# One perceiver layer on one core: denominators of the self attention as a seventeenth value column, normalised on the way out of PSUM, and all engines' steps in a new order

## The reference

```python
q, k = rms_norm(q), rms_norm(k)                       # then rotary, then q * q_gain
scores = einsum('bqhgd,bkhd->bhgqk', qg, k) * scale   # 32 x 32 for a head and sequence
scores = where(causal, scores, -inf)
attn = softmax(scores, axis=-1)
y = einsum('bhgqk,bkhd->bqhgd', attn, v)              # 256 values of a position
return ternary_linear(rms_norm(y), w_proj)
```

## Time and profile before

| what | value |
|---|---|
| three runs, median (lowest, highest) | 593.45 us (590.78, 594.42) |
| the profiled execution, its own time | 593.49 us |
| its span, first to last instruction | 591.3 us |
| TensorE busy | 525.6 us, 89% |
| VectorE, ScalarE, GpSimd busy | 448.9, 424.2, 323.9 us |
| mean granted TensorE clock | 0.958 of 2.4 GHz |

### The profile page before, as it was taken

One profiled execution on the slowest core, in us unless ns is written; L12 is line 12 of the kernel. 1 busy time (PEld: TensorE's weight loads), 2 busy tenths in 40 slices (PEclk: granted clock), 3 DMA queues, 4 the chain that ended last, 5 costly groups with the idle time before them and its releaser, 6 DMA issues. The chain is left out here.

```text
span 591.3 us, 22164 instructions
## 1 busy us (share of the span) xinstructions
PE 525.6 (89%) x6950; PEld 437.1 (74%) x6950; DVE 448.9 (76%) x1389; ACT 424.2 (72%) x1208; POOL 323.9 (55%) x489
## 2 busy tenths in 40 slices
PE   5898989999999999999999999999999999975633
PEld 4686878787887878887887878887877878853422
...
PEclk9999999999999999999999999999999999996565
...
GB/s 249 172 111 76 157 2 112 75 34 97 43 99 54 77 74 63 84 31 115 27 90 54 84 69 70 75 36 118 25 85 53 101 16 99 20 25 7 21 9 9
DMA packets 42748, 41.60 MB, mean 70 GB/s; under 512 B 16080, under 2 KB 33488, under 8 KB 42704
## 3 DMA queue, kind: packets, MB, share of 16 engines
...
...
## 5 line engine op out<-in xcount | busy, mean ns | idle before, releaser
L883 ACT ACTIVATE pr<-sm,nb 128x257 f32<-128x257 f32 x256 | 129.0, 508 | 8.4 <-DVE nb L1122 7.5
L667 POOL TENSOR_TENSOR cTl<-cx,cTh 128x516 fp32r<-128x516 f32 x64 | 85.9, 1342 | 75.9 <-ACT cTh L779 75.9
L1122 DVE CUSTOM_DVE_ANT_0 sm<-x_ps,mbias 128x257 f32<-128x257 f32 x256 | 99.9, 421 | 27.4 <-PE x_ps L1423 24.0
L1433 PE MATMUL x_ps<-tab,pr 128*128 128x128 f32 x512 | 71.6, 274 | 0.7 <-DVE o L1153 0.4
L779 ACT ACTIVATE pt<-x_ps 128x512 f32<-128x512 f32 x112 | 64.9, 594 | 10.2 <-PE x_ps L1433 6.9
L779 ACT ACTIVATE kk<-x_ps 128x257 f32<-128x257 f32 x128 | 49.2, 387 | 29.5 <-PE x_ps L1320 29.5
L1320 PE MATMUL x_ps<-cTh,wkTh 128*128 128x258 f32 x256 | 60.2, 317 | 0.4 <-ACT pt L779 0.3
L1433 PEld LDWEIGHTS x_ps<-tab,pr 128*128 128x128 f32 x512 | 57.2, 141 | 4.4 <-issue 2.0
L676 POOL TENSOR_TENSOR sr<-sv,halfneg 128x20 f32<-128x20 f32 x16 | 56.7, 3543 | 1.3
L1320 PE MATMUL x_ps<-wvTh,cTh 128*128 128x256 f32 x256 | 56.8, 303 | 0.2
L1423 PE MATMUL x_ps<-kk,qbd 32*64 32x257 f32 x1024 | 44.3, 400 | 10.6 <-POOL qbd L688 5.8
...
## 6 DMA issues: line engine op xcount, KB each, us to landing
...
```

Of the source, the lines that this page charges most:

```text
L667: g.tensor_tensor(cxbuf(cT[1], b)[:, :, :], cx[:, b % BT, :, :], cxbuf(cT[0], b)[:, :, :].bitcast(F32), ALU.subtract).then_inc(A_ctl, 1)
L883: sc.activation(pr[:, b % 2, gr, :], sm[:, b % 2, gr, :], ACT.Exp, bias=nb[:, n:n + 1], scale=-1.0, accum_out=st[:, 0, b, gr:gr + 1]).then ...
L1122: v.tensor_tensor_reduce(out=sm[:, b % 2, gr, :], in0=xb(f"S{b}", gr)[:, 0:LK], in1=mbias[:, b, :], scale=1.0, scalar=0.1 * NEG, op0=ALU.a ...
L1433: last = tr(xb(f"PT{b}{c}")[:, gr * P:(gr + 1) * P], pr[:, b % 2, gr, c * P:(c + 1) * P], ident)
```

## The change

The values' block form vbd gets a seventeenth column in each group, which GpSimd fills once, before the passes, with the ones and zeros of the block pattern. The product D_PV is then 68 columns wide in place of 64, and each seventeenth holds the sum of the exponentials. D_dn and D_p3 are gone, with the buffers p3 and dn2; D_p4 transposes p2 itself. A new VectorE step D_ys takes the reciprocals of the 16 sums out of PSUM (strided) and multiplies the 256 values by them from PSUM into ys. ScalarE no longer copies ys; it squares and sums ys from SBUF. The bank of D_PV is free after B_ys in place of B_yss. ScalarE's exponential waits for the transpose (B_p4) of the tile before in place of the product p3. In the files line numbers differ by up to two.

All orders of `SCHEDULE` and the banks of `BANK` are new. Of the tables, the row of GpSimd for one pass, and TensorE's first row:

```diff
@@ SCHEDULE["pool"]["each"] @@
-            ("PX", 0), ("CL", 2), ("CL", 3), ("D_vbd",), ("Q_root",), ("B_root",), ("PX", 1), ("CL", 4),
+            ("CL", 2), ("CL", 3), ("B_root",), ("PX", 0), ("D_vbd",), ("PX", 1), ("CL", 4), ("Q_root",),
...
@@ SCHEDULE["pe"]["each"] @@
-            ("S", 0), ("K", 1, 0), ("K", 1, 1), ("C_xT",), ("B_st",), ("D_kT",), ("V", 1), ("B_O",), ("D_QT",),
+            ("B_st",), ("S", 0), ("K", 1, 0), ("K", 1, 1), ("V", 1), ("C_xT",), ("D_kT",), ("D_QT",), ("PT", 0, 0),
...
@@ perceiver: buffers, release @@
-        vbd = sb("vbd", [P, BT * KV, 4, HD])
-        soft = sb("soft", [P, 5, BT * KV * S])
-        s2, s3, p2, p3, p4 = (soft[:, n, :].rearrange("p (j k) -> p j k", k=S) for n in range(5))
+        vbd = sb("vbd", [P, BT * KV, 4, HD + 1])
+        soft = sb("soft", [P, 4, BT * KV * S])
+        s2, s3, p2, p4 = (soft[:, n, :].rearrange("p (j k) -> p j k", k=S) for n in range(4))
...
-            "D_S": (B_s2, 1, -2, 1), "D_PV": (B_yss, 1, -2, 1), "D_yT": (B_yTl, 1, -2, 1), "D_pj": (B_x2, 1, -2, 1),
+            "D_S": (B_s2, 1, -2, 1), "D_PV": (B_ys, 1, -2, 1), "D_yT": (B_yTl, 1, -2, 1), "D_pj": (B_x2, 1, -2, 1),
@@ GpSimd @@
+            g.tensor_copy(vbd[:, :, :, HD], m4.unsqueeze(1).to_broadcast([P, BT * KV, 4])).then_inc(W_set, 1)
...
                         g.tensor_tensor(
-                            vbd[:, :, :, :],
+                            vbd[:, :, :, 0:HD],
@@ ScalarE @@
                     elif k == "D_S":
                         act.wait_ge(B_s3, i1)
                         if due(i1 - 1):
-                            act.wait_ge(B_p3, i1 - 1)
+                            act.wait_ge(B_p4, i1 - 1)
                         sc.activation(p2[:, :, :], s3[:, :, :], ACT.Exp).then_inc(B_p2, 1)
                     elif k == "D_PV":
-                        act.wait_ge(B_pv, i1)
-                        if due(i1 - 1):
-                            act.wait_ge(B_yTp, i1 - 1)
-                        copy(ys[:, :], xb("D_PV")[:, 0:D]).then_inc(B_ys, 1)
+                        act.wait_ge(B_ys, i1)
                         if due(i1 - 1):
                             act.wait_ge(B_yv, i1 - 1)
-                        sc.activation(ysq[:, :], xb("D_PV")[:, 0:D], ACT.Square, accum_out=yss[:, :]).then_inc(B_yss, 1)
+                        sc.activation(ysq[:, :], ys[:, :], ACT.Square, accum_out=yss[:, :]).then_inc(B_yss, 1)
@@ VectorE @@
-                    elif k == "D_dn":
+                    elif k == "D_p4":
                         dve.wait_ge(B_p2, i1)
-                        v.tensor_reduce(dn2[:, :], p2[:, :, :], AX.X, ALU.add).then_inc(B_dn, 1)
-                        dve.wait_ge(B_dn, i1)
-                        v.reciprocal(rd2[:, :], dn2[:, :]).then_inc(B_rc2, 1)
-                    elif k == "D_p3":
-                        dve.wait_ge(B_rc2, i1)
-                        v.tensor_tensor(p3[:, :, :], p2[:, :, :], rd2[:, :].unsqueeze(2).to_broadcast([P, BT * KV, S]),
-                                        ALU.mult).then_inc(B_p3, 1)
-                    elif k == "D_p4":
-                        dve.wait_ge(B_p3, i1)
                         if due(i1 - 1):
                             dve.wait_ge(B_pv, i1 - 1)
-                        v.transpose(p4[:, :, :].rearrange("p j k -> p (j k)"), p3[:, :, :].rearrange("p j k -> p (j k)")
+                        v.transpose(p4[:, :, :].rearrange("p j k -> p (j k)"), p2[:, :, :].rearrange("p j k -> p (j k)")
                                     ).then_inc(B_p4, 1)
+                    elif k == "D_ys":
+
+                        dve.wait_ge(B_pv, i1)
+                        pv = xb("D_PV")[:, 0:16 * (HD + 1)].rearrange("p (n d) -> p n d", d=HD + 1)
+                        v.reciprocal(rd2[:, :], pv[:, :, HD:HD + 1].rearrange("p n d -> p (n d)")).then_inc(B_rc2, 1)
+                        dve.wait_ge(B_rc2, i1)
+                        if due(i1 - 1):
+                            dve.wait_ge(B_yTp, i1 - 1)
+                        if due(i1 - 1):
+                            dve.wait_ge(B_yss, i1 - 1)
+                        v.tensor_tensor(ys[:, :].rearrange("p (n d) -> p n d", d=HD), pv[:, :, 0:HD],
+                                        rd2[:, :].unsqueeze(2).to_broadcast([P, 16, HD]), ALU.mult).then_inc(B_ys, 1)
@@ TensorE @@
-                                last = mm(xb("D_PV")[b * S:(b + 1) * S, j * 64:(j + 1) * 64], p4[:, b * KV + j, :],
+                                last = mm(xb("D_PV")[b * S:(b + 1) * S, j * 68:(j + 1) * 68], p4[:, b * KV + j, :],
```

More of the change, by code:

```diff
@@ L58 @@
 BANK = {
[L59 to L62, removed]
[3 rows of a table removed]
+    "K10": (4,), "K11": (1,), "V1": (2,), "K20": (6,), "K21": (5,), "V2": (2,), "K30": (1,), "K31": (3,), "V3":
+    (2,), "K40": (5,), "K41": (3,), "V4": (1,), "B_O": (4,), "B_oT": (4,), "B_wo": (1,), "B_xT": (5,), "B_qkv":
+    (5,), "D_QT": (4,), "D_kT": (5,), "D_S": (5,), "D_PV": (6,), "D_yT": (6,), "D_pj": (6,), "C_xT": (3,), "C_z0":
+    (6,), "C_z1": (2,), "C_z2": (0,), "C_hT": (1,), "C_y": (1,), "GATE": (6,), "Q_h": (5,), "Q_q": (5,), "PT00":
[3 rows of a table added]
     "P_k1": (3,), "P_v": (4,), "P_vx": (5,),
@@ L112 @@
+            ("D_pj",), ("PV", 2), ("PT", 3, 0), ("PT", 3, 1), ("V", 4), ("PV", 3),
         ],
         "last": [
[L114 to L117, removed]
@@ new lines @@
+            (16, "B_st"), (16, "C_xT"), (16, "B_O"), (16, "C_z", 0), (16, "B_oT"), (16, "D_kT"), (16, "D_QT"),
+            (16, "B_wo"), (16, "D_S"), (16, "C_z", 1), (16, "B_xT"), (16, "C_z", 2), (16, "B_qkv"), (16, "D_PV"),
+            (16, "D_yT"), (16, "C_hT"), (16, "D_pj"), (16, "C_y"), (17, "C_xT"), (17, "D_QT"), (17, "D_kT"),
+            (17, "C_z", 0), (17, "D_S"), (17, "C_z", 1), (17, "C_z", 2), (17, "D_PV"), (17, "C_hT"), (17, "D_yT"),
+            (17, "C_y"), (17, "D_pj"), (18, "C_xT"), (18, "C_z", 0), (18, "C_z", 1), (18, "C_z", 2), (18, "C_hT"),
@@ L134 @@
+            (18, "C_y"),
         ],
@@ L196 @@
+            (17, "C_z", 2), (17, "D_S"), (17, "C_hT"), (17, "D_PV"), (17, "D_yT"), (18, "C_xT"), (18, "C_z", 0),
             (18, "C_z", 1), (18, "C_z", 2), (18, "C_hT"),
@@ L217 @@
         ],
         "each": [
[3 rows of a table removed]
-            ("S", 2, 2), ("D_dn",), ("B_norm",), ("Q_norm",), ("B_xT",), ("C_z", 0), ("C_h", 0), ("S", 2, 3),
-            ("D_p3",), ("D_p4",), ("S", 3, 0), ("B_qkv",), ("S", 3, 1), ("C_z", 1), ("C_h", 1), ("S", 3, 2),
-            ("C_z", 2), ("C_h", 2), ("C_q", 0), ("C_q", 1), ("C_q", 2), ("S", 3, 3), ("PT", 2, 1), ("D_yT",),
-            ("C_y",), ("D_pj",), ("D_xstats",), ("D_xq", 0), ("D_xq", 1), ("D_xq", 2),
+            ("S", 0, 0), ("S", 0, 1), ("S", 0, 2), ("B_den",), ("S", 0, 3), ("D_scale",), ("B_o1",), ("B_comb",),
@@ new lines @@
+            ("D_kT",), ("B_comb2",), ("Q_stats",), ("B_O",), ("D_S",), ("S", 1, 0), ("B_fin",), ("D_mx",),
+            ("D_s3",), ("S", 1, 1), ("S", 1, 2), ("S", 1, 3), ("B_wo",), ("B_x1",), ("S", 2, 0), ("S", 2, 1),
+            ("B_norm",), ("C_z", 0), ("S", 2, 2), ("C_h", 0), ("S", 2, 3), ("D_p4",), ("B_xT",), ("C_z", 1),
+            ("Q_norm",), ("S", 3, 0), ("S", 3, 1), ("B_qkv",), ("S", 3, 2), ("C_h", 1), ("C_z", 2), ("D_ys",),
+            ("C_h", 2), ("C_q", 0), ("S", 3, 3), ("C_q", 1), ("C_q", 2), ("D_yT",), ("PT", 2, 1), ("C_y",),
@@ L232 @@
-            (14, "B_norm"), (14, "S", 2, 3), (14, "B_xT"), (14, "D_dn"), (14, "C_z", 0), (14, "D_p3"),
-            (14, "C_h", 0), (14, "Q_norm"), (14, "D_p4"), (14, "B_qkv"), (14, "C_z", 1), (14, "S", 3, 0),
-            (14, "C_h", 1), (14, "S", 3, 1), (14, "S", 3, 2), (14, "C_z", 2), (14, "C_h", 2), (14, "C_q", 0),
-            (14, "S", 3, 3), (14, "C_q", 1), (14, "PT", 2, 1), (14, "C_q", 2), (14, "D_yT"), (14, "C_y"),
-            (14, "D_pj"), (14, "D_xstats"), (15, "S", 0, 0), (15, "S", 0, 1), (15, "S", 0, 2), (15, "S", 0, 3),
@@ L247 @@
-            (16, "C_z", 1), (16, "B_wo"), (16, "C_h", 1), (16, "B_x1"), (16, "D_S"), (16, "C_z", 2), (16, "B_norm"),
-            (16, "D_mx"), (16, "D_s3"), (16, "B_xT"), (16, "C_h", 2), (16, "D_dn"), (16, "D_p3"), (16, "D_p4"),
-            (16, "C_q", 0), (16, "C_q", 1), (16, "B_qkv"), (16, "C_q", 2), (16, "D_yT"), (16, "C_y"), (16, "D_pj"),
-            (16, "D_xstats"), (16, "D_xq", 0), (16, "D_xq", 1), (16, "D_xq", 2), (17, "D_scale"), (17, "D_kT"),
-            (17, "C_z", 0), (17, "C_h", 0), (17, "D_S"), (17, "D_mx"), (17, "C_z", 1), (17, "D_s3"), (17, "C_h", 1),
@@ new lines @@
+            (15, "B_fin"), (15, "D_S"), (15, "D_mx"), (15, "S", 1, 3), (15, "C_z", 0), (15, "D_s3"), (15, "B_wo"),
+            (15, "B_x1"), (15, "S", 2, 0), (15, "S", 2, 1), (15, "C_h", 0), (15, "B_norm"), (15, "S", 2, 2),
+            (15, "S", 2, 3), (15, "C_z", 1), (15, "D_p4"), (15, "C_h", 1), (15, "B_xT"), (15, "D_ys"),
+            (15, "S", 3, 0), (15, "S", 3, 1), (15, "S", 3, 2), (15, "S", 3, 3), (15, "C_z", 2), (15, "C_h", 2),
```

(11 more changed lines are left out.)

193 lines of the change are left out of this document (89 added, 104 removed), and 121 rows, old and new, of tables (BANK, SCHEDULE).

## The result

The changed kernel takes 609.37 us in the median of four runs (609.21 to 610.0), against 592.4 us for the kernel before in the same measurements. The ratio is 1.0289, with a 95% interval of 1.0267 to 1.031: slower by 17 us. The forecast was slower, 599.9 us.

What follows compares the result with a forecast made beforehand. The prediction took TensorE to bound the kernel's middle, idle only 1.3 us a pass. Terms -3.0 + 5.1 + 5.5 + 0 + 0.6 - 1.0 - 0.8 = +6.4 us on 593.49 gave 599.9 us; range 584.5 to 606.

Steps and rivals of the forecast that it cites:

- The collision: Passes 3 to 13: GpSimd's vbd holds up VectorE's xn, 2.17 us against 0.33; TensorE waits at B_xT, +5.1 us.
- rival A: Passes 3 to 13: xn gets through before vbd, no added wait; 585 us, or 589; chance 0.28.
- The term for B_qkv, +5.5 us: TensorE at B_qkv waits 0.5 us for the late xnTl in each of eleven passes, +5.5 us.
- C_hT, 0: TensorE's wait at C_hT for quantised hidden values: account even, 0, bounds -3.3 and +5 us over the loop.
- rival C: D_ys on VectorE waits for D_PV and delays C_hT, 0.8 us a pass; 608 us; chance 0.09.
- the head: Loop head: B_st goes first and fills 0.3 us of the wait for qbd, ten passes, -3.0 us.
- rival B: TensorE's waits only move to the next step, and gains and added columns cancel; 593 us; chance 0.10.
- The lists and the tail, -1.8 us: New lists for passes 0 to 2, 14 and 15: -1.0 us; the last tile's chain: -0.8 us.
- D_PV's columns: TensorE's D_PV grows from 64 to 68 columns, 4/64 of about 0.6 us over 16 tiles: +0.6 us.
- D_ys: New VectorE step: reciprocal 253 ns and product 399 ns, 0.65 us, replacing 1.62 us a tile.
- B_fin: On VectorE, no longer beside CL 2: down to 0.42 us, some 0.65 us less; counted as nothing.

Runs made afterwards that it cites:

- the run with four quarters: Changed kernel, its order untouched, with GpSimd's one product vbd written as four products over 128 x 256: 595.78 us.
- experiment 2: Changed kernel with D_vbd moved behind Q_root in GpSimd's order for passes 3 to 13: 594.89 us.
- experiment 5: Changed kernel with B_rope moved ahead of B_qkroot in GpSimd's order for passes 3 to 13: 604.49 us.
- experiment 6: Changed kernel with D_vbd behind Q_root and B_rope ahead of B_qkroot in GpSimd's order for passes 3 to 13: 589.04 us.

## Why the prediction was wrong

Slower was right, and so was the cause that was named; the size was 6.4 us in place of 17. For the eleven passes 3 to 13 the terms summed to 8.2 us (-3.0, +5.1, +5.5, 0 and +0.6), and these passes cost 17.6 + 2.2 = 19.8. By its own steps:

**The collision: right.** xn was to take 2.17 us in eleven passes, and does. TensorE was to wait 0.85 us at B_xT and waits 0.95. The forecast with the collision and rival A without it lay 599.9 - 585.0 = 14.9 us apart; with the collision taken away the chip gives 14.5. That the order of the dispatches does not save xn was the point that decided; the trace has it ahead of vbd by 0.06 us and losing in each of eleven passes. But it is no rule that VectorE loses from there: before, hqb was 0.05 us ahead of ra and won in every pass of the loop. The Trainium skill, "SBUF — State Buffer", section "SBUF: two separate sides", has the shared ports held for a whole instruction, and the run with four quarters agrees (0.84 us in place of 2.17, same place). That section gives the ports to the one that "starts first"; which one that is cannot be read off starts in the profile that lie 0.05 or 0.06 us apart, as xn lost and hqb won.

**The term for B_qkv, +5.5 us: wrong.** No wait for xnTl shows in the after profile. VectorE took 1.98 us from the start of C_z 0 (326.48) to that of xnTl, not 2.27, since operations begin 0.33 to 0.35 us apart and not their length; and TensorE came to B_qkv 2.29 us after B_xT, not 2.06. xnTl ends at 328.84, B_qkv starts at 328.98. So the 14.9 us were in part luck: of the 14.5 measured, B_xT's wait of 0.95 us in 11 passes is 10.4, and the other 4 are not at B_qkv but nearly all in waits that count as busy (0.40 us a pass, experiment 2).

**C_hT, 0: wrong.** I weighed D_ys (rival C) and found the account even. It was even; but the new order lets ra start 0.08 us ahead of hqb, where it had started 0.05 us behind it, and I did not look at this pair. I had asked which GpSimd instruction the new order puts beside xn, and not the same of the other operations of VectorE with both ends in SBUF. It costs 4.9 us (experiment 5).

**Waits that count as busy, no term: wrong, and as large a miss as any.** The prediction took TensorE's busy time as work and added only the columns of D_PV. It rose by 0.58 us a pass, 6.4 us in eleven. Of it 0.40 us go with the collision of xn (experiment 2), and 0.19 us are seen at D_PV's new bank; the two were not separated, and the bank was not put back by itself. The rest of the miss is idle time in small waits: S 1 and S 2 have 0.32 and 0.15 us, B_st 0.17, K 0.16.

**The level of rival A, 585 us: wrong.** With vbd out of the way the kernel takes 594.9, not 585, and with both collisions gone 589.0. I had let every wait that went be a gain: -4.3 at B_xT and -3.0 at the head. Both waits went (qbd from 0.62 to 0.15-0.2 us), but S 1, S 2, S 0 and B_st now wait 0.8 us a pass against 0.17 at S 3 before, and short bank waits hide in the busy time. A pass of the kernel of experiment 6 is 0.19 us shorter than before, where 0.6 was counted. To that extent rival B, that each gap turns up at the next step, was right.

**The lists and the tail, -1.8 us:** -1.0 us in passes 0 to 2 and -2.8 behind the loop, 2 us more than was taken. **D_PV's columns, D_ys, B_fin:** as priced. The granted clock was read as high until about 549 us; the line of the earlier trace rows has it high to some 532. Nothing in the sum hangs on it.
